# Ten blocks of x turned one a step, after the step's sums, and loaded between the chunks of edge features

## The reference

```
src, dst = edge_index[0], edge_index[1]
msg = relu(x[src] + edge_attr @ W_e + b_e)            # 21250 edges, 512 features
aggr = segment_sum(msg, dst, num_segments=x.shape[0]) # edges are sorted by dst
h = (1.0 + eps) * x + aggr                            # 1250 nodes
h = silu(bn(h @ W1 + b1, g1, beta1))
h = h @ W2 + b2
return silu(bn(h, g2, beta2))
```

## Time and profile before

| what | value |
|---|---|
| median of 3 runs | 876.99 us |
| the profiled execution | 880.07 us |
| its span, first to last instruction | 878.2 us |
| mean granted TensorE clock | 0.955 of full |
| TensorE busy | 793.8 us, 90% |
| VectorE busy | 655.6 us, 75% |
| ScalarE busy | 450.3 us, 51% |
| GpSimd busy | 349.9 us, 40% |

### The profile page before, as it was taken

The page is one execution under the profiler, slowest core; times in us unless marked ns, Lnnn a source line. Parts: engine busy times, 40 slices in busy tenths (PEclk is TensorE's granted clock), DMA queues, the critical chain, the costliest instruction groups (busy, mean ns, idle before and its releaser), DMA issues.

```text
span 878.2 us, 11402 instructions
## 1 busy us (share of the span) xinstructions
PE 793.8 (90%) x3714; PEld 628.5 (72%) x3714; DVE 655.6 (75%) x1161; ACT 450.3 (51%) x805; POOL 349.9 (40%) x381
## 2 busy tenths in 40 slices
PE   7398999898969999969679999999999999999993
PEld 6265655555539999958358888878767798989893
DVE  6379999999997973268569999999985362525365
ACT  4377888888864432211157778778753121111122
POOL 6356677777700000011487777777720000000001
PEclk8789999999999999979789999999999999999996
DMA  8759888888820031003668888888831210100011
GB/s 222 261 157 324 262 245 256 251 251 252 265 95 1 1 121 72 1 12 128 204 191 248 264 257 259 263 256 262 263 100 36 72 72 1 72 1 1 1 49 69
DMA packets 49293, 134.38 MB, mean 153 GB/s; under 512 B 8169, under 2 KB 8425, under 8 KB 48848
## 3 DMA queue, kind: packets, MB, share of 16 engines
q0 software_dynamic: 26720, 87.58, 33.1%
q1 hardware_dynamic: 22020, 45.59, 15.2%
q10 hardware_dynamic: 492, 0.45, 0.2%
HBM read 128.47 MB, written 5.12 MB: 152 GB/s over the span
## 4 chain that ended last, share of the span: by engine, by line
PE 62%; DVE 24%; issue 6%; DMA 4%; ACT 2%; POOL 1%; SPq 0%; DVEq 0%; ACTq 0%; POOLq 0%
PE banks L499 36%; PE banks L526 12%; DVE msg_lo L1085 8%; DVE raw L1093 5%; PE banks L552 4%; PE banks L553 4%; DVE attr_hl L1008 3%; DVE hot L1079 3%; DMA attr_sb<-in_attr 2%; DVE agg L1108 1%; PE banks L566 1%; DVE stats L1209 1%; DMA raw<-table_dram,src_sb 1%; PE banks L575 1%; POOL raw L428 1%
## 5 line engine op out<-in xcount | busy, mean ns | idle before, releaser
L428 POOL DMA_INDIRECT raw<-in_x,src_sb x167 | 159.0, 952 | 80.6 <-DVE msg_lo L1085 50.2
L428 POOL DMA_INDIRECT raw<-table_dram,src_sb x167 | 163.0, 976 | 63.7 <-issue 35.8
L552 PE MATMUL banks<-msg_hi,hot 128*128 128x512 f32 x334 | 142.0, 425 | 9.5 <-DVE msg_lo L1085 7.0
L450 POOL TENSOR_TENSOR moments<-moments,minus_half 128x1 f32<-128x1 f32 x32 | 20.3, 635 | 322.7 <-DVE moments L1215 322.7
L869 ACT ACTIVATE msg_hi<-raw 128x512 fp32r<-128x512 f32 x168 | 105.5, 628 | 69.2 <-DVE raw L1093 67.4
L553 PE MATMUL banks<-msg_lo,hot 128*128 128x512 f32 x334 | 132.6, 397 | 0.0
L1093 DVE TENSOR_TENSOR raw<-banks,raw 128x512 f32<-128x512 f32 x168 | 114.2, 680 | 16.1 <-PE banks L526 12.8
L1085 DVE SCALAR_TENSOR_TENSOR msg_lo<-banks,msg_hi 128x512 fp32r<-128x512 f32 x166 | 112.7, 679 | 15.8 <-ACT msg_hi L869 15.8
L830 ACT ACTIVATE banks<-raw 128x512 f32<-128x512 f32 x166 | 98.7, 595 | 44.5 <-DMA raw<-table_dram,src_sb 36.6
L1085 DVE SCALAR_TENSOR_TENSOR msg_lo<-raw,msg_hi 128x512 fp32r<-128x512 f32 x168 | 113.7, 677 | 3.3 <-ACT msg_hi L869 3.3
L552 PEld LDWEIGHTS banks<-msg_hi,hot 128*128 128x128 f32 x334 | 63.8, 191 | 52.6 <-DVE msg_lo L1085 42.9
(11 more groups left out here) (167 smaller groups left out, 1650.9 us busy)
## 6 DMA issues: line engine op xcount, KB each, us to landing
attr_sb<-in_attr SPq DMA_DIRECT2D x84, 128.0 KB, 4.6
attr_sb<-in_attr SPq DMA_DIRECT2D x42, 256.0 KB, 3.9
Wg_raw<-in_Wg SPq DMA_DIRECT2D x3, 1536.0 KB, 6.5
W_raw<-in_W SPq DMA_DIRECT2D x2, 2048.0 KB, 14.1
raw<-in_x,src_sb POOLq DMA_INDIRECT x167, 4.3
raw<-table_dram,src_sb POOLq DMA_INDIRECT x167, 4.1
x_in<-in_x SPq DMA_DIRECT2D x5, 512.0 KB, 10.4
rows<-in_x SPq DMA_DIRECT2D x1, 2560.0 KB, 12.4
```

The source lines that it names most:

```text
L428: pool.indirect_dma_start(rows_of(L, t), None, tables[L], bass.IndirectOffsetOnAxis(ap=src_sb[:, t:t + 1], axis=0)).then_inc(gathered[t % ...
L552: nc.tensor.matmul(acc, h, msg_hi[L][:, t % MSG, :], start=start, stop=False)
```

## The change

`TURN_X` is now a step and no longer a tile, and is 3. Block b is turned in step 3 + b (steps 3 to 12), at the end of PE's step, behind the sums. All blocks go through bank 7, so block b waits until block b-1 has been taken out by ACT. Bank 5 is the sums' alone, and the sums of group 1 no longer wait for the ten blocks. ACT has one `start_sums` in each of these steps. SP asks for chunk 3 of the features first, then for the first two blocks of x, then chunk 4, and so on to chunk 7. The step in which DVE adds the first window to `agg` goes from 8 to 13, since all ten blocks must be there; the count of stray edges goes from step 8 to 14, and its answer from step 10 to 16.

```
-TURN_X = 6
+TURN_X = 3
...
-        start_bank = [bank[5], bank[7]]
+        start_bank = bank[7]
...
             sp.wait_ge(add_mm[0], 1)
-            for q in range(XQ):
-                sp.dma_start(x_in[:, q * XB:(q + 1) * XB, :], by_block[:, q * XB:(q + 1) * XB, :]).then_inc(x_in_done[q], 16)
             for c in range(RING, CHUNKS):
                 load_chunk(0, c)
+                q = c - RING
+                if q < XQ:
+                    sp.dma_start(x_in[:, q * XB:(q + 1) * XB, :], by_block[:, q * XB:(q + 1) * XB, :]).then_inc(x_in_done[q], 16)
                 if c == 3 * RING:
                     sp.dma_start(W1_raw[:, :, :], W1.rearrange("(k p) n -> p k n", p=P)).then_inc(w1_in, 16)
...
                     wait(pe, window_added[L], g - 1)
-                    if L == 0 and g == 1:
-                        pe.wait_ge(agg_start, BLOCKS)
...
                 if b == 0:
-                    pe.wait_ge(pool_consts, 5)
-                elif b == 1:
                     pe.wait_ge(base_copied, 1)
                 else:
-                    pe.wait_ge(agg_start, b - 1)
+                    pe.wait_ge(agg_start, b)
...
                         for t in step_tiles(j):
                             edge_product(L, t)
-                            if L == 0 and 0 <= t - TURN_X < BLOCKS:
-                                turn_x(t - TURN_X)
-                    if L == 0 and j == 8:
+                    if L == 0 and j == TURN_X + BLOCKS + 1:
...
                     if 0 <= j - SUM_LAG < STEPS:
                         for t in step_tiles(j - SUM_LAG):
                             sum_product(L, t)
+                    if L == 0 and 0 <= j - TURN_X < BLOCKS:
+                        turn_x(j - TURN_X)
...
-                    if L == 0:
-                        for t in step_tiles(j):
-                            if 0 <= t - TURN_X < BLOCKS:
-                                start_sums(t - TURN_X)
+                    if L == 0 and 0 <= j - TURN_X < BLOCKS:
+                        start_sums(j - TURN_X)
...
+            def add_step(L, g):
+                step = last_step(g) + SUM_LAG + ADD_AFTER
+                return max(step, TURN_X + BLOCKS) if L == 0 and g == 0 else step
...
-                    if L == 0 and j == 10:
+                    if L == 0 and j == TURN_X + BLOCKS + 3:
                         left_flag()
                     for g in range(GROUPS):
-                        if last_step(g) + SUM_LAG + ADD_AFTER == j:
+                        if add_step(L, g) == j:
                             add_window(L, g)
```

More of the change, by code:

```diff
@@ L582, in turn_x @@
                 if b == 0:
-                    pe.wait_ge(pool_consts, 5)
-                elif b == 1:
                     pe.wait_ge(base_copied, 1)
                 else:
-                    pe.wait_ge(agg_start, b - 1)
+                    pe.wait_ge(agg_start, b)
                 for k in range(KD):
-                    tr = nc.tensor.transpose(start_bank[b % 2][:, k * P:(k + 1) * P], x_in[:, b, k * P:(k + 1) * P], ident[:, :])
+                    tr = nc.tensor.transpose(start_bank[:, k * P:(k + 1) * P], x_in[:, b, k * P:(k + 1) * P], ident[:, :])
                 tr.then_inc(x_turned, 1)
@@ L877, in start_sums @@
                     act.wait_ge(eps_ready, 1)
-                nc.scalar.activation(agg[0][:, :, b * P:b * P + r], feature_major(start_bank[b % 2])[:, :, 0:r], ACT.Identity,
+                nc.scalar.activation(agg[0][:, :, b * P:b * P + r], feature_major(start_bank)[:, :, 0:r], ACT.Identity,
                                      scale=one_eps[:, 0:1]).then_inc(agg_start, 1)
```

## The result

The kernel after takes 864.22 us (median of 4 runs, 862.61 to 866.14), the kernel before 877.30 us (4 runs on the same chip, 876.02 to 877.89). The medians are 13.1 us apart; the ratio is 0.9854 [0.9826, 0.9881], by which it is 12.8 us (10.4 to 15.3). The forecast was 862.0, and 15.0 less; 864.22 lies inside its range (858.5 to 867.5), 2.2 us above the forecast.

What follows compares the result with a forecast made beforehand. DVE was taken to bound steady edge-loop steps at 2.62 us, with a hole while chunk 3 waited behind x. Terms -18.1 + 0.3 + 1.3 + 0.5 + 1.0 = -15.0 us gave 862.0 us, range 858.5 to 867.5.

Steps and rivals of the forecast that it cites:

- The hole: Layer 0's edge loop, 28.30 to 39.20 us: PE and DVE idle awaiting chunk 3; removing it with its tail: -18.1 us.
- the tail: Behind the hole: PE at 0.50 clock, DVE waits of 3.23, 0.21 and 0.74 us, all forecast to go.
- The new costs: Early edge loop: +0.3 for x, +1.3 for gathers, +0.5 for ACT and +1.0 for W1.
- The loads of x, +0.3: First blocks of x behind chunk 3: PE waits 0.5 us, counted +0.3 us; later loads hidden.
- The gathers, +1.3: Steps after the former hole: gathers land later than their lead while x loads, costing +1.3 us.
- ACT, +0.5: Ten steps with one block of x each about fit ACT's spare time, costing +0.5 us (0 to 2.5).
- W1, +1.0: W1's load, asked for at about 46 to 47 us, may meet x's last blocks: +1.0 us (0 to 3).
- The window and the count, 0: `add_window` moved from step 8 to 13 and the stray-edge count moved: same work, 0 us.
- DMA as the bound: Rival: DMA bounds the first twenty steps, gathers getting half the bandwidth; saving 10.2, so 867 us; chance 0.17.
- The clock: Rival: a wait idles PE in steps 3 to 12, clock falls to 0.50; 865 to 869 us; chance 0.04.
- the ring: Slower rival: PE, ACT and DVE wait on each other in every one of ten steps; 879 us; chance 0.03.

Runs made afterwards that it cites:

- Experiment 1: Kernel after with the old queue order (all five loads of x ahead of chunk 3), new turning kept, on slower chips: 965.95 us, ratio 1.0000.
- experiment 12: Kernel after with every load of x made twice and all in front of chunk 3, new turning kept: 881.99 us, ratio 1.0058.
- experiment 8: Kernel before with every load of x made twice, so 5 MB stand in front of chunk 3, on slower chips: 977.89 us, ratio 1.0116.
- experiment 11: Kernel after with ACT writing the block of x behind the chunk's two splits instead of ahead of them: 865.54 us, ratio 0.9876.
- experiment 2: Kernel before with only the new queue order, still turning two blocks a step, on slower chips: 970.44 us, ratio 1.0045.
- experiment 3: Kernel before with chunk 3 alone asked for ahead of the five loads of x, on slower chips: 962.37 us, ratio 0.9997.
- experiment 7: Kernel before, unaltered, profiled on the slower chips: one execution of 972.6 us.

## Why the prediction was right

**The hole** was the term that carried it, and it was right: the wait is gone, and with it the 0.50 clock. Experiment 1 brings a wait of 5.06 us back by the queue's order alone, experiment 12 one of 19.29 us by the order and twice the bytes, and experiment 8 shows that the bytes in front of chunk 3 make it longer. One thing in it was wrong: the prediction gave all of the 18.1 us to the place of chunk 3, "since with it PE's idle time, the slow clock and the tail go too". Experiment 12 still has a hole and yet most of the tail is gone, so the spread turning has a part of it: 1.80 us of waits behind the hole, where the kernel before had 4.18 up to the first calm step.

From step 4 to step 22 the prediction had 69.1 less 15.0, that is 54.1 us; it was 53.01. It is 18.1 saved less 2.0 of new costs, where I had 3.1. That the two sums are so near is in part luck, since the terms missed in both directions.

**The new costs, term by term.**

- *The loads of x, +0.3:* the first load cost nothing in this execution. In experiment 11 PE waited 1.95 us for it. The 2 us of latency in the working of this term no run here shows. I had looked for a wait at the wrong load: "10 us or more for 768 KB, which at the pace above take about 6. Hidden." That pace was mis-sized. The third load took 11.7 us and the fifth 13.4 us to land, in stretches where all queues together moved 330 to 345 GB/s. I had taken the pace from a load asked for when nothing else of SP's was on the way. PE's waits were 0.72 and 0.91 us; only the second reached DVE, as 0.37 us at 48.24, and once more by way of ACT: its block at 47.70 came 0.66 us late from PE, ACT was busy without a gap from there on, and DVE waited 0.41 us for it at 49.94. Together that is 0.78 us.
- *The gathers, +1.3, and ACT, +0.5:* the waits were 0.91, 0.16 and 1.02 us on ACT. The last cost DVE nothing. DVE's other waits for ACT, at 25.27, 30.98 and 38.71, are 0.55 + 0.57 + 0.27 = 1.39 us, where the two terms had 1.8. How they divide isn't shown, since a step with a block and a split fills ACT (5.00 of 5.00 us) whether a gather is late or not.
- *W1, +1.0:* this fell. W1 was asked for at 46.53, as forecast, just as the last of x landed (47.0), and chunk 10 was 1.09 us late for ACT, where it was 1.20 before. DVE lost 0.42 us instead of 1.13. So the term was -0.7 instead of +1.0. It rested on a reading that was wrong, too: before the change the DMA engines were not half empty when W1 was asked for (65.53), but busy for a share of 0.81 from 64 to 68 us.
- *The window and the count, 0:* PE waited 1.35 us for DVE's `add_window` at 54.64, and no edge product was late behind it.

The sum: 1.39 (gathers and ACT) + 0.78 (x) + 0.21 (the wait at 34.75, which was among the 18.1) - 0.71 (chunk 10) + 0.3 (0.8 us without a named wait, where it was 0.5) = 2.0 us.

**DMA as the bound** had 0.17, for 867 us. The DMA view of the kernel after, 20 to 24 us, beside the earlier trace rows:

```profile
q1 hardware_dynamic: 385, 0.69, 55.7%
q0 software_dynamic: 193, 0.66, 48.9%
...
raw<-in_x,src_sb POOLq DMA_INDIRECT x4, 6.8
```

The two queues moved nearly the same bytes, 0.69 and 0.66 MB, where rows 5 had 1.00 and 0.40. The Trainium skill, in "DMA: Bandwidth & Descriptors", section "Queues, rings and completion order", has the engines take turns between the queues a packet at a time. The profile counts 385 and 193 packets here and 515 and 122 in rows 5; whether these are the packets that the page means isn't shown, so the two stretches neither confirm the rule nor contradict it. The consequence that I drew for equal bytes did not come: the gathers took 6.8 us to land here, and the waits behind them cost DVE under 2 us. Their 0.66 MB in 4 us are 165 GB/s, where two gathers of 262 KB in a step of 2.62 us ask for 200, but that only had to last until x was in, and most of it did not reach DVE. That GpSimd's lead covered it is likely and was not tried.

**The clock and the ring** did not come in this execution: the clock stays at 1.00 from 20 to 76 us, and no wait of DVE for ACT is over 0.57 us. The chance of 0.04 for the clock was low, though: in experiment 11, which differs from the change only in ACT's order, PE worked at 0.50 from 25.37 to about 31.4, behind a wait of 1.95 us for x, and DVE lost 1.58 and 1.66 us by it.

**What stays open.** In the pair of profiled executions the change gives 16.1 us between step 4 and step 22, and another 2.2 us before step 4; behind step 22 it is 0.9 us slower. The 2.2 us can't be put down to the change: step 4 came at 23.44 here, at 25.61 before, at 27.45 in experiment 11 and at 25.57 in experiment 12. The medians differ by 13.1 us. The profiled execution of the kernel before (880.07) was slower than all four of its runs, and that of the kernel after the fastest of its four, so the pair overstates the gain. Against the medians the forecast of 15.0 is 1.9 us too much; whether the hole is shorter in the executions of the kernel before that weren't profiled, or the clock falls in some of the kernel after, no trace shows. How the gain divides between the two halves of the change is also open on the first chip: the order alone with the old turning, and chunk 3 alone in front, were run only where the pauses are (experiments 2 and 3).

## What to carry to other kernels

A hole in which all engines stand still while the DMA engines are full is read from the engine that works in order: what does it wait for, and what lay in front of that on its queue? Small loads that are due soon go first, and big ones go between them, in pieces, each with its due step; but then the consumer must be spread too, since the order on the queue alone made the kernel 0.45% slower (experiment 2). The time of the first load on an empty queue can be half of what a later one takes: 5.7 us for 512 KB there, 11.7 and 13.4 us here with the DMA engines full, 6.2 us in experiment 2.

## What the runs showed of the hardware

Ten of the twelve runs came to chips on which this kernel takes about 10% longer, before and after alike. Their mean granted clock is lower (0.927 in experiment 3, 0.955 in the profile of the kernel before on the first chip), but most of the time goes elsewhere. In nearly every group of twelve tiles of the edge loops there is a pause, mostly of about 3.3 us, in which PE, ACT, DVE and GpSimd all stand still; ACT and DVE start again together, PE and GpSimd within 2 us. The timeline of experiment 3:

```profile
123.85 0.60 ACT L831 ACTIVATE sums<-banks 128x512 f32<-128x512 f32 x1 [3.25 <-remote]
123.97 0.69 DVE L1094 TENSOR_TENSOR raw<-banks,raw 128x512 f32<-128x512 f32 x1 [3.27 <-remote]
...
124.50 0.66 PE L576 MATMUL banks<-ident,sums 128*128 128x128 f32 x4 [3.62 <-ACT sums L831]
125.53 0.95 POOL L429 DMA_INDIRECT raw<-in_x,src_sb  x1 [3.56 <-DVE msg_lo L1086]
```

There are two edge loops of 14 groups each, and the 87 us (964 less 877) would be about 26 such pauses. The dense products between and behind the loops have none: behind the second loop the same work of DVE takes 169.0 us in both (754.35 to 923.36 in experiment 3, 670.02 to 839.04 in the kernel before). What makes the pause wasn't found. The same change gives 0.34% there and 1.5% on the first chip. That the pauses give the queues time, and so leave less to gain, fits the shorter hole in experiment 7, but wasn't tried by itself.
